# Edge gather of the second stream: every second indirect gather waits for the landing of the one ahead of it

## The chip, the cores and the metric

The kernel runs on one core of one Trainium2 chip. Its time is the device time of one execution in microseconds (us), smaller is better. The kernel before takes 4981.63 us, the median of three runs (4978.19 to 4985.81).

## The reference

The reference takes node features `x` (6250 nodes, 256 features), a list of 200000 edges for a first graph layer and a list of 131072 edges for a second one. Cut to what matters:

```python
xn = layernorm(x)
x  = x + graph_attention(xn, src, dst)            # 200000 edges, 4 heads of 64
       + linear_attention(xn)                      # 8 heads of 32
y  = layernorm(x)
h  = y @ W_gat                                     # 16 columns: 4 heads x 4 experts
e  = leaky_relu(a_src[src] + a_dst[dst])           # 131072 edges and one loop per node
alpha = exp(e - max over dst) / sum over dst
scores = layernorm(segment_sum(h[src] * alpha, dst) + b).mean over heads
out = x + sum over 4 experts of gate(scores) * (gelu(y @ W1[e] + b1[e]) @ W2[e] + b2[e])
```

The change concerns `h[src]` and `a_src[src]` of the second graph layer: one row of 20 numbers (16 of `h`, 4 of `a_src`) is fetched for every edge.

## The kernel before

The program runs through stages that follow one another. First the edges are sorted and tables built; then comes the first stream, which fetches a row of 264 numbers for each edge of the first graph with 1612 indirect gathers and sums them by destination. A third group of stages computes the nodes' features for the second layer and sorts its edges. Then comes the second stream (`edge_stream`, L2109 to L2401), and last the gates and the weighted sum of the experts.

The second stream works on 1216 chunks of 128 edges, in 38 bundles of `SPAN` = 32 chunks. For each chunk, GpSimd (POOL) issues one indirect gather (L1929) of 128 rows of 20 floats, one row to each partition, into a ring of `GATHERED` = 6 bundle slots in SBUF. Each slot has a semaphore of its own, `got[slot]`, which each landed gather raises by 16. POOL does nothing else in this stream: its whole program there is one call of `EdgeGather.share`. The first `AHEAD` = 112 gathers (3.5 bundles) are issued in the stage ahead of the stream by `EdgeGather.ahead`, which calls `share` in lots of 8; the other 1104 are issued in the stream itself (L2212).

Two waits hold POOL back in `share`. At the first chunk of a bundle it waits until the slot is free again, that is, until VectorE has done `scale` (L2335) of the bundle six back (semaphore `scaled`). And each gather of bundle `j` waits until all 32 gathers of bundle `j - 2` have landed.

What uses the rows: for each bundle, VectorE waits for `got[slot]` and adds the two scores (`pack`, L2311), TensorE turns them (L2221), VectorE runs the maximum over runs of equal destinations (`shift`, L2321 to L2328), ScalarE takes the exponential (L2276), TensorE turns back (L2228), ScalarE copies out (L2282), VectorE multiplies the gathered rows by the weights (`scale`, L2335), and TensorE sums the rows of each chunk with a one-hot matrix (L2238). VectorE then combines the chunks' sums (`align`, `combine`). Between these steps TensorE, ScalarE and VectorE work on a fixed list of steps of the four experts' dense layers (`Experts`, L2043 to L2106), 12 steps in each bundle; the order on each engine is written out by hand. SyncE loads the run marks (`resets`, L2184) and stores the experts' rows (L2023) and the states of each bundle (L2189).

Of the kernel before, what the change touches and what calls it, by code (L numbers as in the profile page):

```python
# [27 lines left out]
WIDE = E2 // P + BLOCK  # L28
SPAN = 32
GATHERED = 6  # L30
BUNDLES_AT_ONCE = 2
EDGE_CHUNKS = 1216
EDGE_GRID = 1280
# [1289 lines left out]
def stream(nc, kept, c, sem, d, g, e, x, wqkv, wout, gamma, key_max):  # L1323
# [8 lines left out]
    GAP = P - 1 + LOW  # L1332
    AT_ONCE = BUNDLES_AT_ONCE
    assert NB % AT_ONCE == 0
# [387 lines left out]
class UnitScatter:  # L1722
# [9 lines left out]
    def share(self, pool, n):  # L1732

        for u in range(self.done, self.done + n):
            lot, v = u // LOT, u - self.first
            if lot >= 2:
                pool.wait_ge(self.scattered[(lot - 2) % 3], 16 * LOT * ((lot - 2) // 3 + 1))
            pool.indirect_dma_start(  # L1738
                out=self.out, out_offset=bass.IndirectOffsetOnAxis(ap=self.unit[:, v:v + 1], axis=0),
                in_=self.keys[:, v * UNIT:(v + 1) * UNIT], in_offset=None, bounds_check=ROOM - 1,  # L1740
                oob_is_err=False).then_inc(self.scattered[lot % 3], 16)
        self.done += n
# [162 lines left out]
class EdgeGather:  # L1905


    def __init__(self, nc, kept, c, d, g, e):
        self.rows, self.src, self.chunks, self.done = d[g.tag + "_rows"], e.src, g.chunks, 0
        self.out = kept.enter_context(nc.sbuf_tensor(g.tag + "_gathered", [P, GATHERED, SPAN, 20], F32))  # L1910
        self.got = [c.held.enter_context(nc.semaphore("%s_rows_got%d" % (g.tag, k))) for k in range(GATHERED)]

# [7 lines left out]
    def share(self, pool, n, scaled=None):  # L1920

        end = min(self.chunks, self.done + n)
        for k in range(self.done, end):
            j, u = divmod(k, SPAN)
            if j >= GATHERED and u == 0:
                pool.wait_ge(scaled, j - GATHERED + 1)
            if j >= 2:
                pool.wait_ge(self.got[(j - 2) % GATHERED], 16 * SPAN * ((j - 2) // GATHERED + 1))
            pool.indirect_dma_start(out=self.out[:, j % GATHERED, u, :], out_offset=None, in_=self.rows,  # L1929
                                    in_offset=bass.IndirectOffsetOnAxis(ap=self.src[:, k:k + 1], axis=0)  # L1930
                                    ).then_inc(self.got[j % GATHERED], 16)
        self.done = end
# [924 lines left out]
```

## Time and profile before

| what | us |
|---|---|
| median of three runs | 4981.63 |
| the profiled execution, from its first to its last instruction (its span) | 6245.5 |
| busy in the profiled execution: TensorE matmul | 3399.7 |
| VectorE | 2946.1 |
| ScalarE | 1902.2 |
| GpSimd | 3158.9 |
| gathers of the first stream (L1440), busy, 1612 of them | 1603.5 |
| gathers of the second stream (L1929), busy, 1216 of them | 1201.9 |
| GpSimd idle just before gathers of L1929 | 1249.8 |

The profile is of one execution, and that one took 6245.5 us where the three timed runs took 4978 to 4986. The page shows no time for it but the span, so the span is its own time. A row of the page's groups gives the line, the engine, the operation, what it writes and reads, the count, then busy us and mean ns of one, then the idle time of the engine just before these instructions with what released it. The busy time of a gather on POOL is the making of its descriptors; when its data land is another time. PEclk is the granted clock of TensorE as a share of full speed.

### The profile page before, as it was taken

How to read it: one execution, taken by the hardware profiler on the slowest of the kernel's cores; microseconds unless marked ns; L12 is line 12 of the kernel's file. 1: busy time of each engine (PE TensorE's matmuls, PEld its weight loads, DVE VectorE, ACT ScalarE, POOL GpSimd, SP SyncE). 2: the span in 40 equal slices, each digit the busy share in tenths (PEclk: the TensorE clock that was granted, in tenths of full speed). 3: DMA queues.
4: the chain of work that ended last, by engine and by line, in shares of the span. 5: the costliest groups of instructions: out<-in, count | busy, mean ns of one | idle time of the engine just before them, and what ended most of it. 6: DMA issues, size and time to landing. Idle time of an engine off the chain costs nothing. (4 is left out here: it accounts for less than half of the span.)

```text
span 6245.5 us, 58318 instructions
## 1 busy us (share of the span) xinstructions
PE 3399.7 (54%) x14771; PEld 2497.0 (40%) x14771; DVE 2946.1 (47%) x6874; ACT 1902.2 (30%) x6108; POOL 3158.9 (51%) x3144
## 2 busy tenths in 40 slices
PE   5554356565666666655552634555455554555660
PEld 4454244444444444443342523334334343343450
DVE  8765455555566666665564722122222222222336
ACT  4100244444456566655441001111111111111220
POOL 0176666665666566656644673544444545445200
PEclk8655677777767777777765556677677776777765
DMA  3265333333333334333321631111111113334216
GB/s 109 74 207 166 104 93 95 95 96 91 95 101 106 105 106 109 106 100 96 93 76 52 223 109 24 26 26 27 24 25 31 23 30 24 25 31 22 30 34 248
DMA packets 326836, 508.54 MB, mean 81 GB/s; under 512 B 102092, under 2 KB 249219, under 8 KB 314654
## 3 DMA queue, kind: packets, MB, share of 16 engines
q0 software_dynamic: 126320, 232.73, 19.0%
q1 hardware_dynamic: 190334, 266.01, 13.0%
q10 hardware_dynamic: 9900, 6.68, 0.3%
q8 instruction: 100, 1.64, 0.1%
q14 instruction: 182, 1.48, 0.1%
HBM read 425.57 MB, written 79.71 MB: 81 GB/s over the span
## 5 line engine op out<-in xcount | busy, mean ns | idle before, releaser
L1440 POOL DMA_INDIRECT gnn_gathered<-gnn_rows,gnn_src x1612 | 1603.5, 995 | 970.2 <-issue 454.4
L1929 POOL DMA_INDIRECT ffn_gathered<-ffn_rows,ffn_src x1216 | 1201.9, 988 | 1249.8 <-DVE ffn_scaled L2335 807.9
L1528 PE MATMUL gnn_step_ps<-gnn_scaled,gnn_dst_onehot 128*128 128x260 f32 x3224 | 1209.8, 517 | 820.2 <-DVE gnn_scaled L1622 585.3
L1467 ACT ACTIVATE gnn_scaled<-gnn_gathered,gnn_edge_weights 128x65 f32<-128x65 f32 x4464 | 1137.4, 336 | 778.2 <-remote 377.5
L1528 PEld LDWEIGHTS gnn_step_ps<-gnn_scaled,gnn_dst_onehot 128*128 128x128 f32 x3224 | 746.7, 252 | 1122.6 <-DVE gnn_scaled L1622 674.2
L1642 DVE TENSOR_TENSOR gnn_sums<-gnn_sums,gnn_step_ps 128x260 f32 x1612 | 680.5, 422 | 623.9 <-PE gnn_step_ps L1528 252.0
L2054 PE MATMUL exp_hidden_ps<-exp_xn_turned,exp_w 128*128 128x512 f32 (+1 forms) x832 | 532.5, 777 | 486.4 <-ACT exp_hidden L2085 342.5
L2238 PE MATMUL ffn_sum_ps<-ffn_scaled,ffn_dst_onehot 128*128 128x24 f32 x2432 | 392.6, 320 | 350.6 <-issue 234.3
L2085 ACT ACTIVATE exp_hidden<-exp_hidden_ps,exp_b 128x512 f32<-128x512 f32 (+1 forms) x208 | 137.8, 663 | 1304.9 <-remote 750.5
L2238 PEld LDWEIGHTS ffn_sum_ps<-ffn_scaled,ffn_dst_onehot 128*128 128x128 f32 x2432 | 392.0, 254 | 356.5 <-issue 235.1
L2054 PEld LDWEIGHTS exp_hidden_ps<-exp_xn_turned,exp_w 128*128 128x128 f32 x832 | 189.8, 253 | 659.0 <-ACT exp_hidden L2085 365.6
L2062 PE MATMUL exp_out_ps<-exp_w,exp_hidden 128*128 128x256 f32 x1568 | 416.9, 414 | 0.0
L2062 PEld LDWEIGHTS exp_out_ps<-exp_w,exp_hidden 128*128 128x128 f32 x1568 | 341.9, 219 | 168.7 <-issue 126.0
L2305 DVE TENSOR_TENSOR ffn_dst_onehot<-ffn_local_dst,iota_row 128x1024 f32<-128x1024 f32 x152 | 183.0, 1224 | 430.2 <-DMA gnn_bundle_ends<-gnn_step_ends 322.8
L2106 DVE TENSOR_TENSOR exp_out<-exp_out_ps,exp_b 128x256 f32<-128x256 f32 x196 | 80.7, 421 | 487.0 <-PE exp_out_ps L2062 361.5
L1738 POOL DMA_INDIRECT ffn_keys<-edges_sorted,edges_unit_place x192 | 226.7, 1181 | 77.6 <-issue 57.7
L2074 ACT COPY exp_xn_turned<-exp_turn_ps 128x256 f32<-128x256 f32 x49 | 18.3, 372 | 769.2 <-PE exp_turn_ps L2043 767.6
L1558 DVE TENSOR_TENSOR gnn_dst_onehot<-gnn_local_dst,iota_row 128x1664 f32<-128x1664 f32 x124 | 236.7, 1909 | 0.1
L2321 DVE TENSOR_TENSOR_SCAN ffn_maximum_until<-ffn_resets_of_rows,ffn_row_ps 128x128 f32<-128x128 f32 x38 | 15.9, 418 | 416.3 <-remote 394.4
L1622 DVE TENSOR_TENSOR gnn_scaled<-gnn_gathered,gnn_edge_weights 128x260 f32<-128x260 f32 x496 | 209.6, 423 | 2.5 <-issue 1.2
L2348 DVE TENSOR_SCALAR ffn_missing<-ffn_sum_ps 128x64 f32<-128x64 f32 x76 | 16.8, 221 | 378.1 <-DMA gnn_bundle_ends<-gnn_step_ends 315.0
L1738 POOL DMA_INDIRECT ffn_keys<-mid_late_keys,mid_late_unit x102 | 113.3, 1110 | 87.8 <-DMA mid_late_unit<-late_unit 57.0
(424 smaller groups left out, 4469.6 us busy)
## 6 DMA issues: line engine op xcount, KB each, us to landing
nn_local_rows_everywhere<-gnn_local_rows SPq DMA_DIRECT2D x52, 1024.0 KB
fn_local_rows_everywhere<-ffn_local_rows SPq DMA_DIRECT2D x40, 1024.0 KB
gnn_gathered<-gnn_rows,gnn_src POOLq DMA_INDIRECT x1612
expert_rows<-exp_out SPq DMA_DIRECT2D x196, 128.0 KB
sum_expert_rows<-expert_rows SPq DMA_DIRECT2D x12, 2048.0 KB, 16.8
ffn_gathered<-ffn_rows,ffn_src POOLq DMA_INDIRECT x1216
ffn_kept_states<-ffn_states SPq DMA_DIRECT2D x38, 384.0 KB
mix_xn_transposed<-xn_transposed SPq DMA_DIRECT2D x98, 128.0 KB
```

The source lines that it names most:

```text
L1440: pool.indirect_dma_start(out=G[:, n, u, :], out_offset=None, in_=d[t + "_rows"], in_offset=bass.IndirectOffsetOnAxis(ap=e.src[:, st:st + ...
L1467: last = act.activation(ZW[:, st % BUF, h * F:(h + 1) * F], G[:, i % 2, u, h * F:(h + 1) * F], ACT.Copy, scale=W[:, i % 2, h, u:u + 1])
L1528: pe.matmul(ps[:, st % BUF, 0:g.row], OH[:, st // PIECE % 2, u % PIECE, :], ZW[:, st % BUF, :], start=True, stop=True).then_inc(multiplied, 1)
L1558: dve.tensor_tensor(OH[:, piece % 2], bcast(e.dst[:, cut].unsqueeze(2), [P, PIECE, P]), bcast(c.row[:].unsqueeze(1), [P, PIECE, P]), ALU.i ...
L1622: dve.tensor_tensor(ZW[:, st % BUF, :].rearrange("p (h f) -> p h f", h=H), G[:, i % 2, u, 0:g.row].rearrange("p (h f) -> p h f", h=H), bca ...
L1642: dve.tensor_tensor(to, to, ps[:, st % BUF, 0:g.row], ALU.add).then_inc(added, 1)
L1738: pool.indirect_dma_start(out=self.out, out_offset=bass.IndirectOffsetOnAxis(ap=self.unit[:, v:v + 1], axis=0), in_=self.keys[:, v * UNIT: ...
L1929: pool.indirect_dma_start(out=self.out[:, j % GATHERED, u, :], out_offset=None, in_=self.rows, in_offset=bass.IndirectOffsetOnAxis(ap=self ...
L2054: last = pe.matmul(self.PH[:, 0:w], self.W1[:, e, k, q * P:(q + 1) * P], self.XT[:, i % 2, k, 0:w], start=k == 0, stop=k == 1)
L2062: last = pe.matmul(self.PO[:, n % 2, 0:D], self.HT[:, e % 2, h, q * P:(q + 1) * P], self.W2[:, e, h, :], start=h == 0, stop=h == self.HC - 1)
L2238: last = pe.matmul(ps[:, u // HALF, u % HALF * COLS:(u % HALF + 1) * COLS], OH[:, u // PIECE % 2, u % PIECE, :], ZW[:, u, :], start=True, ...
L2305: dve.tensor_tensor(OH[:, q % 2], bcast(e.dst[:, cut].unsqueeze(2), [P, PIECE, P]), bcast(c.row[:].unsqueeze(1), [P, PIECE, P]), ALU.is_eq ...
```

## The change

Inside the second stream (where `scaled` is given), a gather at an even place `u` of its bundle now waits until the gather directly ahead of it, `k - 1`, has landed; the first of the stream is left out, since the one ahead of it belongs to the stage before. The gathers at odd places keep the wait on the bundle two back. The gathers of the stage ahead of the stream (`ahead`, which passes no `scaled`) are as they were. No instruction is added or removed on any other engine.

```diff
+PAIR = 2
...
             j, u = divmod(k, SPAN)
             if j >= GATHERED and u == 0:
                 pool.wait_ge(scaled, j - GATHERED + 1)
-            if j >= 2:
+            if scaled is not None and u % PAIR == 0 and k > self.done:
+                b, v = divmod(k - 1, SPAN)
+                pool.wait_ge(self.got[b % GATHERED], 16 * (SPAN * (b // GATHERED) + v + 1))
+            elif j >= 2:
                 pool.wait_ge(self.got[(j - 2) % GATHERED], 16 * SPAN * ((j - 2) // GATHERED + 1))
             pool.indirect_dma_start(out=self.out[:, j % GATHERED, u, :], out_offset=None, in_=self.rows,
                                     in_offset=bass.IndirectOffsetOnAxis(ap=self.src[:, k:k + 1], axis=0)
```

## Rows read from the trace of the kernel before

**Rows 1.** Busy time by stretch: us, then PE, PEld, DVE, ACT, POOL, PEclk, DMA share, GB/s.
```profile
0.00:622.00 622.00, 339.92 (x2804) 291.12 (x2804) 439.72 (x1032) 101.91 (x283) 240.13 (x213) 0.63 0.43 139
622.00:3172.00 2550.00, 1502.65 (x4896) 1069.54 (x4896) 1523.17 (x3794) 1313.23 (x4802) 1603.49 (x1612) 0.74 0.37 99
3172.00:3640.00 468.00, 226.23 (x2027) 193.58 (x2027) 303.98 (x676) 69.99 (x306) 248.89 (x215) 0.54 0.39 128
3640.00:5840.00 2200.00, 1147.85 (x4251) 798.29 (x4252) 481.74 (x944) 350.09 (x599) 1065.43 (x1103) 0.70 0.22 28
5840.00:6061.00 221.00, 183.01 (x795) 144.50 (x794) 92.55 (x178) 61.16 (x113) 0.97 (x2) 0.77 0.10 31
6061.00:6245.00 184.00, 0.00 (x0) 0.00 (x0) 104.99 (x252) 5.84 (x7) 0.00 (x0) 0.50 0.63 218
```

**Rows 2.** Waits on POOL: who waited for whom, us in total, times, longest us.
```profile
POOL ffn_gathered L1929 <- DVE ffn_scaled L2335: 807.9, 31, 46.8
...
POOL gnn_gathered L1440 <- DVE gnn_scaled L1622: 449.3, 154, 8.2
POOL ffn_gathered L1929 <- issue: 360.4, 1182, 0.3
```

**Rows 3.** The gathers by line: count, min/median/max ns, first and last start.
```profile
L1929 POOL DMA_INDIRECT ffn_gathered<-ffn_rows,ffn_src x1216: 941/947/1977, 3456.0 to 5840.3; - x174
...
L1440 POOL DMA_INDIRECT gnn_gathered<-gnn_rows,gnn_src x1612: 942/949/2653, 622.2 to 3171.1; - x180
```

**Rows 4.** The step `scale`, L2335: while gathers are issued, and after the last gather.
```profile
L2335 DVE TENSOR_TENSOR ffn_scaled<-ffn_gathered,ffn_edge_weights x32: 683/684/691, 3685.3 to 5800.3; 128x512 f32<-128x512 f32 x32
...
L2335 DVE TENSOR_TENSOR ffn_scaled<-ffn_gathered,ffn_edge_weights x6: 683/684/684, 5871.3 to 6040.6; 128x512 f32<-128x512 f32 x6
```

**Rows 5.** Timeline of one bundle's turn (start us, us, engine, line), POOL and DVE.
```profile
4535.70 0.95 POOL L1929 DMA_INDIRECT ffn_gathered<-ffn_rows,ffn_src  x1 [0.30 <-issue]
...
4558.78 0.69 DVE L2335 TENSOR_TENSOR ffn_scaled<-ffn_gathered,ffn_edge_weights 128x512 f32<-128x512 f32 x1
...
4559.74 0.94 POOL L1929 DMA_INDIRECT ffn_gathered<-ffn_rows,ffn_src  x1 [23.09 <-DVE ffn_scaled L2335]
...
4560.98 0.95 POOL L1929 DMA_INDIRECT ffn_gathered<-ffn_rows,ffn_src  x1 [0.30 <-issue]
```

**Rows 6.** Stretches behind the gather of 4535.70, columns as in rows 1.
```profile
4537.00:4537.50 0.50, 0.00 (x0) 0.00 (x0) 0.00 (x0) 0.00 (x0) 0.00 (x0) 1.00 0.22 17
4537.50:4537.80 0.30, 0.00 (x0) 0.00 (x0) 0.00 (x0) 0.00 (x0) 0.00 (x0) 0.57 0.05 7
4537.80:4541.00 3.20, 0.00 (x0) 0.00 (x0) 0.00 (x0) 0.00 (x0) 0.00 (x0) 0.50 0.00 0
```

**Rows 7.** Timeline: turned scores and `shift` beside gathers, then without gathers.
```profile
4514.35 0.27 PE L2221 MATMUL ffn_row_ps<-identity,ffn_scores 128*128 128x128 f32 x1
...
4541.50 0.42 DVE L2321 TENSOR_TENSOR_SCAN ffn_maximum_until<-ffn_resets_of_rows,ffn_row_ps 128x128 f32<-128x128 f32 x1 [20.48 <-remote]
4541.55 0.69 ACT L2085 ACTIVATE exp_hidden<-exp_hidden_ps,exp_b 128x512 f32<-128x512 f32 x1 [14.09 <-remote]
...
5921.79 0.27 PE L2221 MATMUL ffn_row_ps<-identity,ffn_scores 128*128 128x128 f32 x1
...
5922.17 0.42 DVE L2321 TENSOR_TENSOR_SCAN ffn_maximum_until<-ffn_resets_of_rows,ffn_row_ps 128x128 f32<-128x128 f32 x1 [3.31 <-PE ffn_row_ps L2221]
```

**Rows 8.** The last gather of all, and the stretches behind it.
```profile
5840.33 0.95 POOL L1929 DMA_INDIRECT ffn_gathered<-ffn_rows,ffn_src  x1 [0.30 <-issue]
...
5843.00:5843.50 0.50, 0.00 (x0) 0.00 (x0) 0.00 (x0) 0.00 (x0) 0.00 (x0) 0.50 0.76 12
5843.50:5844.00 0.50, 0.00 (x0) 0.00 (x0) 0.00 (x0) 0.00 (x0) 0.00 (x0) 0.50 0.01 0
5844.00:5845.00 1.00, 0.00 (x0) 0.00 (x0) 0.00 (x0) 0.00 (x0) 0.00 (x0) 0.50 0.00 0
```

**Rows 9.** Two stretches of 200 us of the second stream, columns as in rows 1.
```profile
4400.00:4600.00 200.00, 109.65 (x401) 76.82 (x401) 45.56 (x89) 32.75 (x56) 92.08 (x96) 0.70 0.13 26
...
5200.00:5400.00 200.00, 109.22 (x409) 76.11 (x410) 46.84 (x91) 33.90 (x61) 93.27 (x96) 0.72 0.46 26
```

## The prediction, made before the changed kernel was run

> **What bounds the kernel now.** I read the busy time by stretch first [rows 1]. The second stream's gathers fill 3640 to 5840: 2200 us, in which no engine is busy for more than 1148. The waits on POOL come next [rows 2]: it stood 807.9 us before 31 gathers until VectorE had done `scale`, which frees a slot of the ring. So in this trace the gathers are not late; the other engines are. The starts of `scale` say by how much [rows 4]: (5800.3 - 3685.3) / 31 = 68.2 us a bundle while gathers are issued, (6040.6 - 5871.3) / 5 = 33.9 us after the last one. The timeline shows where the difference lies [rows 7]. TensorE turned the scores at 4514.35 and VectorE's scan of them began at 4541.50, with ScalarE let go within 0.1 us of it, 5.8 us after POOL's last gather had started [rows 5]; without gathers the same hand-over took 0.38 us (5921.79 to 5922.17).
>
> Taken alone, this speaks for the change: space the bursts out, and the others run. But the profiled execution took 6245.5 us and the timed runs 4981.6, 1264 less, so not all of its stalls can be in the timed runs, and I have to find what they leave. Work outside the two streams' gathers: 622 + 468 + 184 [rows 1], and of the 221 us after the last gather about 48, one bundle's 33.9 and the closing steps, since six bundles had piled up only because the others were late: 1322 us. That leaves 4982 - 1322 = 3660 us. The first stream issues 1612 gathers, and from one to the next POOL needs 0.95 us of work and 0.30 of issue, 1.25 together (4559.74 to 4560.98) [rows 3, 5]: at least 2015 us. So the second stream's 1104 gathers have at most 3660 - 2015 = 1645 us, where the trace has 2200; at 1.25 us each they need at least 1380, or 40 us a bundle. Without the stalls the others need 33.9 us a bundle, less than POOL's 40. My reading is therefore that in the timed runs **POOL's issue paces the second stream**. Between the floors (2015 + 1380 = 3395) and 3660 lie 265 us that I can't place. I give the second stream 60 of them and the first the rest: the first has a ring of two bundles and POOL waits there for VectorE 154 times, 449.3 us [rows 2], and its VectorE, TensorE and ScalarE are busy 1523, 1503 and 1313 us [rows 1], while the second has six slots. So the second stream's gathers take about 1440 us now.
>
> The Trainium skill says otherwise of the two times: "Runtime: NRT & Kernel Launch", section on the preamble and postamble, has a gap of about 6.2 us between a profile's total and the reported time, whatever the kernel. By it the timed runs would hold all the stalls of the trace. The gap here is 1264 us, so the measurement decides against it; what the stalls would mean if they were real is the second rival below.
>
> **The change part by part.** It removes the wait on the bundle two back from 551 gathers (even places, numbers 114 to 1214). That wait never held: no group of POOL's waits at L1929 names a landing [rows 2], so its removal is worth nothing. The 0.30 us between gathers stays. The 112 gathers of the stage ahead are untouched.
>
> It adds 551 waits for the landing of the gather just issued. What stands behind each on POOL is only the next gathers; who waits for those is `pack` on VectorE, and through it the whole bundle. The price of a pair:
>
> - From the even gather to the odd one nothing changes: 1.25 us.
> - From the start of the odd gather to its landing. The gather that started at 4535.70 is the last of a burst with the other transfers quiet. DMA work goes on through 4537.50 and into the next 0.3 us, and is nil from 4537.80 [rows 6]: landing 1.8 to 2.1 us after the start. For the stores of the experts' rows and states that run beside some gathers I take 2.1.
> - From the landing to POOL's next start. The nearest row is a wait for VectorE: `scale` ended at 4558.78 + 0.69 = 4559.47 and POOL started at 4559.74 [rows 5]: 0.27.
>
> Together 1.25 + 2.1 + 0.27 = 3.62 us, where two gathers take 2.50 now. A bundle then takes 16 x 3.62 = 57.9 us on POOL. The others need 33.9, and they are hidden behind it; if TensorE, with longer pauses, were granted the lower of its clocks (0.50 in idle stretches of rows 6) they would need more, but 24 us of cover are left. The lead of 3.5 bundles is used up either way. Nothing late is cured, since nothing on the other engines is late in the timed runs.
>
> The sum: 552 pairs x 3.62 = 1998 us, less 1440, is +558. The landings can't all be at the quiet value, so I round up to +570: 4982 + 570 = **about 5550 us**. Against the profiled execution's own 6245.5 the sum is another: its 68.2 us a bundle would be replaced by 57.9 if the spaced gathers no longer hold the others up, 10.3 x 34.5 = 355 us less, and by about the same 68 if they do. I expect a span of 5900 to 6400 there, a profile that looks equal or better beside timed runs that are worse.
>
> Bounds of the unknown terms. The wait can't cost less than nothing if the landing came with the end of the descriptors (1.25 + 0.95 + 0.27 = 2.47 a pair, against 2.50), and no row has a landing so early. Above: the last gather of all started at 5840.33 and DMA work goes on until about 5843.5 [rows 8], a landing after 3.1 us; and from 5200 us on the DMA share is 0.46 for the same 26 GB/s that had 0.13 before [rows 9], so landings were longer there. With 3.1 a pair takes 4.62, 2550 us in all, +1110. I stay near the quiet value because two thirds of the stream's stretch have it.
>
> The trace shows the landing at 2.0 us with the DMA engines at 0.05 to 0.22 of their time [rows 6] and 3.1 with them at 0.76 [rows 8]. The Trainium skill, "DMA: Bandwidth & Descriptors", section on latency, has the access to HBM at 0.2 us on average and 2 us at high load, and says that lighter load makes the fixed cost smaller. By that rule the spaced gathers would see shorter landings; what this gives is the third rival.
>
> **The rivals.**
>
> 1. *Long landings.* The state of rows 9 (share 0.46 for the same bytes) belongs to the chip and not to the trace, and holds for a third of the stream or more: 184 pairs x 1.0 us more, +184 and up, with all pairs +552: 5730 to 6100, say 5850. For it: those rows. Against it: the row at 4400 has the same load at 0.13. Chance 0.12.
> 2. *The stalls are real, and the change cures them* (the other side). If the bursts hold TensorE's results back in the timed runs too, a bundle takes more than POOL's 40 us now, and it decides from where it takes more than 57.9. At the trace's 68.2 against 57.9 the change brings 355 us: 4630. For it: [rows 4, 7]. Against it: 68.2 x 34.5 = 2350 us doesn't fit into the 1645 left, unless POOL's work on a gather is also drawn out in the trace; then both streams shrink in proportion (3660 / 4750 = 0.77), 68.2 becomes 52.5, and 57.9 becomes 44.6: 270 us less, 4710. Chance 0.08.
> 3. *Short landings.* With nothing recorded and only two gathers under way, the landing comes 1.5 us after the start, midway between the 0.95 us of descriptors and the 2.1: 3.02 a pair, 1667 us, +227: 5210 (up to 5300 with 1.6). For it: a landing gets shorter where the DMA engines are idle [rows 6, 8]. Against it: rows 6 is already idle. Chance 0.15.
> 4. *It does nothing.* The timed runs' bundle is held at about 58 us by something that no row shows, and POOL's new pace hides behind it: 4980. For it only the 265 us that I couldn't place; against it that 58 x 34.5 = 2000 exceeds 1645. Chance 0.04.
>
> **How the numbers follow.** The forecast has 0.61 and its own range is 5400 to 5700 (landings of 1.85 to 2.35 us: 552 x 0.25 = 138 to either side, rounded up). Rivals 1 and 3 lie on the same side of no change, so the range takes in most of both: 5230 to 5850. Beyond it are rivals 2 and 4 and the far end of 1, about 0.18. Slower by over 0.2% (10 us, about what timing of this kernel can tell from nothing): 0.61 + 0.12 + 0.15 = 0.88. Faster: 0.08. Within 0.2%: 0.04.
>
> **What the profile after would show.** If I am right: POOL's starts at L1929 come in pairs 3.5 to 3.7 us long; its idle time there is put down mostly to landings of `ffn_gathered`, 551 times at 1.3 to 1.6 us, some 800 us; the 807.9 us of waits for `scale` shrink to less than 400; and `pack` (L2311) waits for gathers in bundles after the third. The rest of the kernel, first stream included, stays as it is. I would be wrong at the pair's price if the pairs in the trace last over 4.2 or under 3.1 us. I would be wrong in the reading of the timed runs if they come out under 5000: then the stalls of rows 7 were theirs too. The same is shown if the timed difference is much less than the pairs' sum.

## The result, and the profile after

The changed kernel took 5928.27 us (5925.25 to 5941.01, 4 runs), the kernel before beside it 4979.91 (4971.53 to 4985.81): ratio 1.1913, interval 1.1891 to 1.1936. That is 948 us slower. The forecast was 5550, 570 slower; the direction was right, and the time lies above the range of 5230 to 5850. A ratio is taken over all the runs of a series but those over 1.5% above the fastest, so it can differ a little from the quotient of the two medians.

Everything below needs one fact first. The series were run on several chips, and **the chips are of two kinds for this kernel**. The kernel before took 4979.91, 4976.24 and 4973.44 us in three series and 6369.83, 6254.88 and 6263.32 in three others. Ratios are always taken within one series. I call them the quick and the slow chips. Each of the five series below had a chip of its own and stayed on one of the two levels throughout; that it is the chip, and nothing else that differed between the series, is the plainest reading and was not tested by itself. The result above is from a quick chip. The profiled execution of before (6245.5) fits a slow one.

The profile after spans 5939.0 us, and that same execution was timed at 5941.01. The waits on POOL, columns as in [rows 2]:
```profile
POOL ffn_gathered L1933 <- DMA ffn_gathered<-ffn_rows,ffn_src: 1153.7, 551, 5.9
POOL gnn_gathered L1441 <- issue: 419.1, 1375, 0.3
...
POOL ffn_gathered L1933 <- issue: 202.0, 663, 0.3
...
POOL gnn_gathered L1441 <- DVE gnn_scaled L1623: 68.0, 67, 1.7
```
All 551 added waits held, 2.09 us each, where I had foreseen 1.3 to 1.6. The 807.9 us of waits for `scale` are gone, and so are most of the 449.3 us in the first stream, which the change doesn't touch. That second fact can't come from the edit.

The gathers by line, as in [rows 3], and then, from the page's list of DMA issues, their median us from issue to landing:
```profile
L1933 POOL DMA_INDIRECT ffn_gathered<-ffn_rows,ffn_src x1216: 939/945/2299, 3108.8 to 5713.1; - x174
...
L1441 POOL DMA_INDIRECT gnn_gathered<-gnn_rows,gnn_src x1612: 941/947/2672, 606.7 to 2825.1; - x180
```
```profile
ffn_gathered<-ffn_rows,ffn_src POOLq DMA_INDIRECT x1216, 2.5
```
The same time for the gathers issued from 3295 to 4900 us alone, then from 5000 to 5713:
```profile
DMA to landing us min/median/max: 2.2/2.4/7.0
```
```profile
DMA to landing us min/median/max: 3.1/3.2/5.1
```
Pairs in the timeline of POOL, as in [rows 5], and two stretches, columns as in [rows 1]:
```profile
4302.19 0.94 POOL L1933 DMA_INDIRECT ffn_gathered<-ffn_rows,ffn_src  x1 [1.64 <-DMA ffn_gathered<-ffn_rows,ffn_src]
4303.44 0.94 POOL L1933 DMA_INDIRECT ffn_gathered<-ffn_rows,ffn_src  x1 [0.30 <-issue]
4306.09 0.94 POOL L1933 DMA_INDIRECT ffn_gathered<-ffn_rows,ffn_src  x1 [1.70 <-DMA ffn_gathered<-ffn_rows,ffn_src]
```
```profile
4200.00:4400.00 200.00, 104.58 (x409) 73.59 (x408) 48.65 (x99) 33.34 (x57) 96.58 (x99) 0.70 0.14 26
5400.00:5600.00 200.00, 106.47 (x411) 78.97 (x411) 44.04 (x85) 32.05 (x55) 79.23 (x80) 0.68 0.16 24
```
This pair takes 3.90 us, of which 2.65 go from the odd gather's start to the next start, where I had 2.1 + 0.27. Over 200 us there are 99 gathers in the one stretch (4.04 us a pair) and 80 in the other (5.0): the late part of the stream is slower. After this odd gather, of 4303.44, the last DMA work shows between 4305.4 and 4305.6, and POOL starts again at 4306.09 (columns as in [rows 1]):
```profile
4305.40:4305.60 0.20, 0.00 (x0) 0.00 (x0) 0.00 (x0) 0.00 (x0) 0.00 (x0) 1.00 0.02 3
4305.60:4305.80 0.20, 0.00 (x0) 0.00 (x0) 0.00 (x0) 0.00 (x0) 0.00 (x0) 1.00 0.00 0
```
`pack` now waits for gathers in 32 bundles, 1229.6 us in all, as foreseen. The second stream runs from 3295.05 to 5713.1, 2418 us; I had 1998.

The hand-over of [rows 7], TensorE's turned scores to VectorE's scan: what VectorE stood before it, us and times, in all 38 bundles.
```profile
  PE ffn_row_ps L2225: 11.3, 3
```

### The profile page after: what moved, and what is told of

Its sections match the earlier page's. It is cut to its first block and busy times, and to the rows that moved or that the text cites. A ratio compares the mean times of both kernels' runs of the same rounds, so it can differ in the third digit from the quotient of the medians.

```text
span 5939.0 us, 58318 instructions
## 1 busy us (share of the span) xinstructions
PE 3176.8 (53%) x14771; PEld 2356.0 (40%) x14771; DVE 2929.5 (49%) x6874; ACT 1890.0 (32%) x6108; POOL 3276.4 (55%) x3144
## 5 line engine op out<-in xcount | busy, mean ns | idle before, releaser
L1933 POOL DMA_INDIRECT ffn_gathered<-ffn_rows,ffn_src x1216 | 1238.1, 1018 | 1433.5 <-DMA ffn_gathered<-ffn_rows,ffn_src 1153.7
L1441 POOL DMA_INDIRECT gnn_gathered<-gnn_rows,gnn_src x1612 | 1680.4, 1042 | 546.4 <-issue 419.1
L1529 PE MATMUL gnn_step_ps<-gnn_scaled,gnn_dst_onehot 128*128 128x260 f32 x3224 | 1109.9, 481 | 633.8 <-DVE gnn_scaled L1623 536.5
L1529 PEld LDWEIGHTS gnn_step_ps<-gnn_scaled,gnn_dst_onehot 128*128 128x128 f32 x3224 | 685.6, 232 | 909.6 <-DVE gnn_scaled L1623 645.0
L2315 DVE TENSOR_TENSOR ffn_score_sums<-ffn_gathered,ffn_dst_score_of_edge 128x128 f32<-128x128 f32 x38 | 15.8, 415 | 1229.8 <-DMA ffn_gathered<-ffn_rows,ffn_src 1229.6
L2225 PE MATMUL ffn_row_ps<-identity,ffn_scores 128*128 128x128 f32 x38 | 17.2, 453 | 1032.6 <-DVE ffn_scores L2319 1032.6
L2058 PE MATMUL exp_hidden_ps<-exp_xn_turned,exp_w 128*128 128x512 f32 (+1 forms) x832 | 491.3, 724 | 29.5 <-ACT exp_hidden L2089 17.2
L2242 PEld LDWEIGHTS ffn_sum_ps<-ffn_scaled,ffn_dst_onehot 128*128 128x128 f32 x2432 | 367.9, 243 | 8.9 <-DVE ffn_scaled L2339 6.6
L2242 PE MATMUL ffn_sum_ps<-ffn_scaled,ffn_dst_onehot 128*128 128x24 f32 x2432 | 365.8, 311 | 6.0 <-DVE ffn_scaled L2339 6.0
```

Of the source, the lines that this page charges most:

```text
L1441: pool.indirect_dma_start(out=G[:, n, u, :], out_offset=None, in_=d[t + "_rows"], in_offset=bass.IndirectOffsetOnAxis(ap=e.src[:, st:st + ...
L1529: pe.matmul(ps[:, st % BUF, 0:g.row], OH[:, st // PIECE % 2, u % PIECE, :], ZW[:, st % BUF, :], start=True, stop=True).then_inc(multiplied, 1)
L2058: last = pe.matmul(self.PH[:, 0:w], self.W1[:, e, k, q * P:(q + 1) * P], self.XT[:, i % 2, k, 0:w], start=k == 0, stop=k == 1)
L2242: last = pe.matmul(ps[:, u // HALF, u % HALF * COLS:(u % HALF + 1) * COLS], OH[:, u // PIECE % 2, u % PIECE, :], ZW[:, u, :], start=True, ...
```

## The experiments

**First series, a quick chip** (before: 4976.24, 4966.23 to 4994.33). *e1_before_again* is the kernel before with nothing changed, for its profile.

> The kernel before, unchanged, for a second profile of it. The trace of the changed kernel has its span at its timed value (5939 us against 5928) and its first stream 346 us shorter than the trace of before (gathers from 607 to 2825, against 622 to 3171), though the first stream is the same code. Theory A (in the timed runs POOL's issue paces the second stream): a trace at the timed value of 4980 us has the 1104 gathers of the second stream at 1.25 to 1.35 us each, 1380 to 1490 us from first to last (5941 - 2418 for the changed kernel's stretch = 3523 for the rest, and 4980 - 3523 = 1457), VectorE's scan L2321 follows TensorE's L2221 within about 1 us, and POOL waits little for ffn_scaled. Theory B (the stalls of the first profile are in the timed runs as well): the stretch is near 2200 us again and POOL waits about 800 us for ffn_scaled L2335.

*e2_every_fourth*:
```
-PAIR = 2
+PAIR = 4
```


> The wait for the gather ahead stands at every fourth gather (275 waits) instead of every second (551). Theory A (each wait exposes one landing and the restart of POOL, and POOL paces the stream): in the changed kernel a pair took 4.08 us up to gather 880 and 4.9 us behind it, 1.58 and 2.4 us over 2.50, so half the waits cost half of the sum: 188 x 1.58 + 88 x 2.4 = 508, less the slack of about 75 us that the kernel before has on POOL: 4980 + 430 = 5410, between 5370 and 5480. Theory C (the price is set by how few gathers are under way, not by the number of waits): the two of four that are under way at once still leave the DMA engines idle and the time stays over 5700.

*e3_three_back* (against the changed kernel; two counters for each slot, filled by alternate pairs, and `pack` waits for both):
```
...
-            if scaled is not None and u % PAIR == 0 and k > self.done:
-                b, v = divmod(k - 1, SPAN)
+            if scaled is not None and u % PAIR == 0 and k - 2 > self.done:
+                b, v = divmod(k - 3, SPAN)
...
```


> Same count of waits as in the change (550), each for the landing of the gather three back instead of the one ahead (each bundle slot gets two semaphores so that the wait is exact; pack waits for both). Theory A (what costs is the exposed landing): the gather three back started 3.75 us earlier, and landing takes 2.1 to 2.9 us and the restart about 0.5, so the wait holds POOL almost nowhere: 4980 us, at most 60 us more from the filler gathers at the end of the stream. Theory D (any wait on a landing stops POOL's sequencer and costs its restart, however far back the gather): 550 x about 0.5 us, 5200 us or more, up to the 5928 of the change.

*e4_no_landing_wait* (against the kernel before):
```
-            if j >= 2:
+            if j >= 2 and scaled is None:
```


> The kernel before without the wait on the bundle two back inside the second stream (only the ring's wait for ffn_scaled is left there). Theory A: that wait never holds, the time is the same within 0.3%, 4965 to 4995 us. Rival E: the wait on two bundles back throttles POOL in the filler gathers of the last third or protects the other engines: then the time moves by more than 20 us, in either direction.

Measured: e1 4987.12 (one run, span 4985.2); e2 5481.05, ratio 1.1015 (1.0986 to 1.1044); e3 5018.24, 1.0072 (1.0046 to 1.0097); e4 4976.15, 0.9997 (0.9984 to 1.0009).

e1, gathers by line with what the engine idled for, then POOL's waits:
```profile
L1929 POOL DMA_INDIRECT ffn_gathered<-ffn_rows,ffn_src x1216: 940/944/3306, 3102.5 to 4758.6; - x174
...
  issue: 370.0, 1214
```
```profile
POOL gnn_gathered L1440 <- issue: 422.5, 1387, 0.3
...
POOL gnn_gathered L1440 <- DVE gnn_scaled L1622: 71.1, 64, 1.9
```
There is no wait for `scale` at all: POOL goes from gather to gather with only the 0.30 us of issue. From 3288.41 to 4758.6 it needs 1470 us for the 1104 gathers, 1.33 each, where I had 1440. So on this kind of chip the reading "POOL's issue paces the stream" is shown, and 2418 - 1470 = 948 us, the whole difference of the result. e4 shows that the removed wait was worth nothing on such a chip. e3 keeps just as many landing waits, each two gathers older; of those, only 97 still held:
```profile
POOL ffn_gathered L1934 <- DMA ffn_gathered<-ffn_rows,ffn_src: 59.2, 97, 3.5
```
It costs 42 us, not 948. The price is the exposed landing and not the wait instruction. In e2, 275 waits held:
```profile
POOL ffn_gathered L1933 <- DMA ffn_gathered<-ffn_rows,ffn_src: 600.4, 275, 5.6
```
505 / 275 = 1.84 us a wait, beside 948 / 551 = 1.72 in the change: the cost goes with the number of exposed landings. The 5481 of e2 lies at the end of its expected range (5370 to 5480).

**Second series** asked why the late pairs are longer; in the profile after they lengthen at about gather 875 (3.9 to 4.0 us before it, 4.7 to 5.1 from 880 on). The reference's edge list runs over 8192 node numbers, of which 6250 exist, so only about 100000 edges are kept, and by the program's sorting the row numbers from about gather 856 on are filler, all 0: the 128 descriptors of a gather read one row. No run read the row numbers out; e5 and e7 test them by their effect. It fell on a slow chip (before: 6369.83, 6317.7 to 6431.77). *e5_change_spread_rows*, and *e6_before_spread_rows* the same edit in the kernel before:
```
-                                    in_offset=bass.IndirectOffsetOnAxis(ap=self.src[:, k:k + 1], axis=0)
+                                    in_offset=bass.IndirectOffsetOnAxis(ap=self.src[:, k - 400 * (k >= 832):k - 400 * (k >= 832) + 1], axis=0)
```


> The change, but from chunk 832 on the gathers take the row numbers of the chunk 400 ahead of them, so that each fetches 128 different real rows; the chunks from about 856 on hold filler edges, whose row numbers are all 0, so all 128 descriptors of such a gather read one row. (The kernel so computes with other rows for some real edges of chunks 832 to about 856.) In the changed kernel a gather took 2.03 to 2.07 us up to chunk 880 and 2.40 to 2.49 behind it. Theory F (128 reads of one address land later): the tail runs at 2.04 too, 336 gathers x 0.42 = 141 us less: 5790 us, 5770 to 5815. Theory G (what is slow in the tail has to do with the place in the stream, the tables or the time): unchanged, 5928.

> The same other row numbers from chunk 832 on in the kernel before. There nothing waits closely for a landing: both theories have the time unchanged at 4976 within 0.3%, while by theory F the landings of the last third (3.6 us behind the start, by the transfers' records of the second profile) fall to 2.1 to 2.3 and the DMA share there falls back to that of the middle; by theory G they stay. If the time falls by more than 15 us, the filler gathers cost POOL something in the kernel before as well (its descriptors took 1.03 to 1.08 us there, 1.02 elsewhere).

*e7_change_one_row*: the changed kernel, the second stream's `self.src[:, k:k + 1]` always column 1215, filler. *e8_wait_at_every_gather*: `PAIR = 1`.

> The change with every gather of the stream (from 112 on) fetching the filler chunk's row numbers, so that all gathers read one row 128 times (the sums of the second layer are computed from the wrong rows). Theory F: each of the 756 gathers ahead of the tail costs 2.46 us instead of 2.04, +318: 6245 us. Theory G: 5928 still.

> The wait for the gather ahead at every gather, 1103 waits. Theory A (each wait exposes the landing and costs about the same, whatever the others do): a lone gather is 2.55 to 2.65 us from start to next start in the first two thirds and 3.4 in the tail: 756 x 2.6 + 348 x 3.4 = 3149 us against 1470, so 4976 + 1680 = 6655 us, 6550 to 6800. If the price per wait grew because two gathers landed together in the change (theory H: of a pair's landing, part is queueing behind the first one), the landing of a lone gather is shorter, 2.2 us or less from start to start: below 6300.

Measured: e5 6233.57, 0.9802 (0.9749 to 0.9855); e6 6369.96, 1.0000 (0.9958 to 1.0042); e7 6683.27, 1.0499 (1.043 to 1.0567); e8 7296.65, 1.1462 (1.1393 to 1.1531). Stretches of e5, then of e7, columns as in [rows 1]:
```profile
4200.00:4400.00 200.00, 106.96 (x413) 74.71 (x411) 45.73 (x89) 33.44 (x57) 99.26 (x101) 0.70 0.13 27
5400.00:5600.00 200.00, 106.84 (x406) 74.98 (x407) 49.14 (x101) 32.74 (x56) 98.99 (x100) 0.69 0.13 26
```
```profile
4200.00:4400.00 200.00, 105.25 (x399) 75.66 (x398) 41.39 (x74) 32.74 (x56) 80.29 (x82) 0.67 0.17 25
```
With real rows the late stretch is as quick as the early one (100 and 101 gathers); with filler the early one is as slow as the late one was (82). The longer landing of 128 reads of one row is shown, 0.8 us a pair; the landings of 2.4 and 3.2 us in the profile after say the same. In e8 each of 1103 waits held, 2226.8 us in all, and its second stream took 3304 us, 1.66 us a wait over the 1470 of e1. e5 and e6 fetch other rows for the real edges from gather 832 on too, and e7 fetches the filler's rows for every edge of the stream, so none of the three computes the reference's sums.

e5 and e7 were told as ratios to a before of about 4976, and here the before was 6370. e6's POOL rows show what is different on such a chip:
```profile
POOL ffn_gathered L1929 <- DVE ffn_scaled L2335: 804.0, 31, 47.1
POOL gnn_gathered L1440 <- DVE gnn_scaled L1622: 521.7, 152, 8.0
```
They are [rows 2] again, and this kernel's timed runs are at 6370 too. The stalls are in timed runs here. So the change itself had to be run on a slow chip.

**Third series, a slow chip** (before: 6254.88, 6209.82 to 6296.62): the change, `PAIR = 4`, and e5 and e6 once more.

> The change, unchanged. The same kernel before took 4976 us on the chip of the first experiments and 6370 us on that of the second ones, and the change with spread rows came out 2.0% faster than the kernel before there. Where the kernel before takes about 4976: 5928 again. Where it takes about 6370: the pair of gathers is as long as ever (2.04 us a gather, 2.45 in the filler tail), so the change is the spread version (6233) plus 336 x 0.42 = 141: 6375 us, no different from the kernel before (theory J: the change puts a pace of 65 us a bundle in the place of stalls that cost as much). If the landing waits cost more there (theory K), it is over 6450.

> The wait at every fourth gather. Where the kernel before takes 4976: 5481 again. Where it takes 6370, POOL's pace would be 54.3 us a bundle (62 in the tail) against the 66 at which the kernel before runs. Theory L (what holds TensorE's results back is a long unbroken row of gathers; any gap lets them through): 34.5 x 11 = 380 us less, less the pile-up at the end that goes too: 5850 to 6000 us. Theory M (it goes by the gathers' mean rate, and at 54 us a bundle they are still held back): 6200 us or more.

> The change with 128 different rows in place of the filler's one row. Where the kernel before takes 4976: 5928 - 141 = 5787 us (5770 to 5815), the same 141 us that the gathers' pace in the tail (2.03 us instead of 2.45) gave in the profile of its first run. Where it takes 6370: 6233 again.

> The kernel before with 128 different rows in the tail. Where the kernel before takes 4976: POOL's descriptors set the pace and the landings are hidden, 4976 within 0.3%; landings of the last third fall from 3.6 to about 2.1 us. Where it takes 6370: 6370 again.

Measured: f1 6273.16, **1.003** (0.9993 to 1.0067); f2 5854.24, **0.9381** (0.9286 to 0.9476); f3 6160.92, 0.9841 (0.9754 to 0.9927); f4 6249.8, 0.9992 (0.9953 to 1.0031). f1 was expected at 6375 and f3 at 6233, both worked out from the chip of the second series, which is slower still. The gathers of f1 by line, and POOL's waits:
```profile
L1933 POOL DMA_INDIRECT ffn_gathered<-ffn_rows,ffn_src x1216: 938/945/2405, 3442.7 to 6041.2; - x174
```
```profile
L1441 POOL DMA_INDIRECT gnn_gathered<-gnn_rows,gnn_src x1612: 940/947/2658, 609.8 to 3158.9; - x180
```
```profile
POOL ffn_gathered L1933 <- DMA ffn_gathered<-ffn_rows,ffn_src: 1150.9, 551, 5.5
...
POOL gnn_gathered L1441 <- DVE gnn_scaled L1623: 435.1, 150, 7.9
```
The changed second stream costs POOL the same on both kinds (1150.9 us of landings here, 1153.7 there). What f1 has over the profile after is the untouched first stream: 2549 against 2218 us, 331 of the 345 between the two medians. Against the kernel before on such a chip [rows 3], the second stream has 2414 us (3627 to 6041) in place of 2200, and after the last gather come 227 us in place of 405, since no bundles pile up: +214 - 178 = +36 of some 6260, close to the +18 measured. In f4 the late stretch has DMA share 0.13, where the filler rows of [rows 9] had 0.46 for the same 26 GB/s, yet the time is the same; there the landings are hidden.
```profile
5400.00:5600.00 200.00, 110.17 (x406) 76.63 (x407) 46.08 (x90) 34.43 (x62) 93.38 (x96) 0.70 0.13 26
```

**Fourth series, a slow chip** (before: 6263.32, 6250.23 to 6283.69): `PAIR = 8` (h1) and `PAIR = 16` (h4), the kernel of e3 (h2), and h3, the kernel before with the gathers from the seventh bundle on cut to 64 of 128 partitions (`self.out[0:64, ...]`, `self.src[0:64, ...]`), which leaves the other half of the rows stale.

> The landing wait at every eighth gather, 137 waits. Where the kernel before takes 4976: 137 x 1.84 = 250 more, 5225. Where it takes about 6250: POOL's pace would be 48.5 us a bundle. Theory L (any gap lets TensorE's results through): 34.5 x 6 = 200 us less than with every fourth (5854): 5650. Theory N (only short rows do, results are held after about 8 us of unbroken gathers, as in the first profile): stalls come back and the time is over 5850.

> The landing wait at every sixteenth gather, 69 waits. Where the kernel before takes 4976: 5100. Where it takes about 6250: theory L 5550 (POOL's pace 45.6 us a bundle); theory N near 6000 to 6250.

> 550 waits for the gather three back. Where the kernel before takes 4976: 5018 again. Where it takes about 6250: by the rate of gathers, which these waits leave as it is (1.34 us a gather), nothing is let through, 6250; if the mere presence of a landing wait in POOL's queue were what helps, below 5900.

> The kernel before, but in the stream every gather from bundle 6 on fetches rows for partitions 0 to 63 alone, so half the row transfers with the same number of gathers and of semaphore increments (the other half of the rows is left stale). Where the kernel before takes about 6250: theory Q (what is in the way is the traffic of row transfers and their descriptors): stalls all but go, below 5700. Theory R (it is the gathers and their semaphore increments as such): stalls stay, within 200 us of 6250. Where it takes 4976: POOL's descriptors get shorter, and the stream ends at the 34 us a bundle that the other engines need: 4980 - 31 x 9 = 4700, or 4976 if a gather's 1.3 us do not depend on its rows.

Measured: h1 5606.24, **0.8969** (0.8927 to 0.9011); h4 5955.92, 0.9462 (0.9368 to 0.9556); h2 6166.95, 0.9859 (0.9801 to 0.9918); h3 6215.68, 0.9929 (0.9901 to 0.9957). POOL's waits in h1, h4 and h2:
```profile
POOL ffn_gathered L1933 <- DMA ffn_gathered<-ffn_rows,ffn_src: 321.2, 132, 5.6
```
```profile
POOL ffn_gathered L1933 <- DVE ffn_scaled L2339: 421.3, 24, 28.4
...
POOL ffn_gathered L1933 <- DMA ffn_gathered<-ffn_rows,ffn_src: 104.4, 43, 5.0
```
```profile
POOL ffn_gathered L1934 <- DVE ffn_scaled L2341: 710.8, 31, 45.5
```
And what VectorE stood before the scan of [rows 7], in e6 (no gaps), in h4 (one gap in sixteen) and in h1 (one in eight):
```profile
  remote: 343.7, 20
```
```profile
  remote: 80.7, 17
```
```profile
  PE ffn_row_ps L2225: 14.6, 5
```
The scan's is one hand-over of several. ScalarE's wait for TensorE's results of the experts (`exp_hidden`) in the second stream's gathers, in before, h4, h3 and h1 (`remote`: the view names no instruction that let it go):
```profile
ACT exp_hidden L2085 <- remote: 750.5, 39, 32.9
```
```profile
ACT exp_hidden L2089 <- remote: 633.9, 44, 42.0
```
```profile
ACT exp_hidden L2085 <- remote: 546.8, 26, 41.5
```
```profile
ACT exp_hidden L2089 <- PE exp_hidden_ps L2058: 549.0, 129, 20.4
```
So on a slow chip TensorE's results are handed over late while gathers are issued in long rows, and a landing wait in every eighth gather ends nearly all of it. One in sixteen ends most of the scan's delay but little of ScalarE's, and its time lies between the two that were expected (5550; 6000 to 6250). Below eight the gaps themselves become the bound again. Each wait of h1 costs POOL 321.2 / 132 = 2.43 us, and its bundles take 48 to 51 us (52 to 55 in the filler) in place of 65 in the mean. Waits three back (h2) help by 1.4% only, again between what was expected (6250; below 5900). Only 51 of them held, 40 of these in the filler from gather 880 on, and there alone its bundles are shorter: 55 to 63 us, where before has 63 to 71. With half the rows in each gather (h3) the kernel still stands at 0.993, and POOL waits 801.9 us for `scale` as before, though the scan's own `remote` wait is down to 62.3 us. So what counts is the number of gathers and not the bytes, and the scan's wait alone is a poor measure of the stalls.

**Fifth series, a quick chip** (before: 4973.44, 4971.55 to 4976.47). *i1_both_streams_eighth*: `PAIR = 8`, and in the first stream
```
+                    if st and u % PAIR == 0:
+                        b, v = divmod(st - 1, S)
+                        pool.wait_ge(got[b % 2], 16 * (S * (b // 2) + v + 1))
```
*i2_pause_no_wait*: the kernel before, with a pause of POOL that waits for no landing (the wait is for the pause before it):
```
+            if scaled is not None and u % 8 == 0:
+                if self.paused:
+                    pool.wait_ge(self.rested, self.paused)
+                pool.memset(self.idle[:], 0.0).then_inc(self.rested, 1)
+                self.paused += 1
```


> Landing waits at every eighth gather of the second stream, as before, and at places 0, 8, 16 and 24 of each bundle of 26 in the first stream (247 more). Its gathers move 13 times the bytes, so a wait there costs 2 us or more. Where the kernel before takes about 6260: the first stream's gathers took 2620 us there and 2211 us where the kernel takes 4976; the waits cost 247 x 2 = 494 us of POOL's time and can give back up to 409: about 5690 us, between 5550 and 5800, no gain over 5606. If the first stream's stalls are of another kind, 6000 or more. Where the kernel before takes 4976: 5225 + 450 = 5675.

> The kernel before with a memset of 128 x 1024 floats on POOL ahead of every eighth gather of the second stream (138 of them), into a tile that nothing reads, and no new landing wait. A memset of about 1 us and the hand-over leave a pause of some 1.5 us between gathers, in which the last gather lands only in part. Where the kernel before takes about 6260: if a pause of POOL is what lets the results through, about 5600 to 5700; if the gathers have to have landed, 5950 or more. Where it takes 4976: 138 x 1.5 = 207 more, 5180.

Measured: i1 5790.21, 1.1646 (1.1623 to 1.1668); i2 5084.65, 1.0224 (1.0204 to 1.0244). POOL's waits in i1 and its timeline in i2:
```profile
POOL gnn_gathered L1444 <- DMA gnn_gathered<-gnn_rows,gnn_src: 527.2, 201, 3.8
...
POOL ffn_gathered L1936 <- DMA ffn_gathered<-ffn_rows,ffn_src: 324.5, 137, 5.1
```
```profile
4001.55 0.94 POOL L1936 DMA_INDIRECT ffn_gathered<-ffn_rows,ffn_src  x1 [0.30 <-issue]
4002.49 0.97 POOL L1932 MEMSET ffn_idle<- 128x1024 f32 x1
4003.62 0.95 POOL L1936 DMA_INDIRECT ffn_gathered<-ffn_rows,ffn_src  x1 [0.16 <-issue]
```
Both were meant for a slow chip and fell on a quick one, where there is no stall to cure. They show the costs alone: an exposed landing in the first stream (201 of them, 2.62 us of POOL's idle time each, where I had expected 2) and a pause of 0.8 us (111 / 138, where I had 1.5). Whether a pause without a wait frees a slow chip was not measured.

## Why the prediction was wrong, by its own steps

- **"In the timed runs POOL's issue paces the second stream", about 1440 us.** Right for the chip of the result: 1470 (e1), and the first stream has 2212 there where the sum leaves it 2220.
- **The removed wait is worth nothing.** Right on a quick chip: e4, 0.9997.
- **551 added waits, a landing exposed in each.** Right: 551 in the profile after. e3 shows that the landing is what costs.
- **Start of the odd gather to its landing, 2.1 us: the step that failed.** This term of the pair's price was too small for every pair. I took it from the last activity of the DMA engines [rows 6]. In the profile after that activity ends at about 2.1 us as well (4303.44 to 4305.5), but POOL starts again only 0.5 us later and not 0.27. With real rows a gather lands 2.4 us after its issue in the median (2.2 at the least), and from the odd gather's start to the next start the median is 2.65 where I had 2.37. Over 551 waits that is 154 us. In the filler the landing takes 3.2 us.
- **"The landings can't all be at the quiet value", rounded up by 12 us, and the upper bound of 3.1 given to a third of the stream only as rival 1.** The mean wait was 2.09 us where my sum has 1.42 (2.37 - 0.95): 369 us over 551 waits. Of these, 154 are the step above, about 145 the filler rows (168 pairs at 4.93 us against 4.08; e5 and e7), and the other 70 single longer landings, some 30 of them in the first four bundles; what lengthens those no run took apart. The descriptors, at 0.99 us in the mean and not 0.95, add 44. 369 + 44 = 413 of the 420 by which the stream's 2418 exceeds 1998. The forecast itself missed by less, 378, since the stream had 1470 before and not 1440 and I had rounded up by 12. [Rows 9] had shown the filler stretch, and I read it as a rival instead of as a term. The 3.1 us of [rows 8] is a filler gather too: I put its length down to the share of 0.76, and it is what filler takes at 0.16. Rival 1's time (5730 to 6100) was the right one, and its mechanism in half: the long landings are real for a third of the stream, but they belong to the row numbers and not to the chip.
- **Rival 3, short landings.** Wrong: the least one is 2.2 us. The rule of the Trainium skill ("DMA: Bandwidth & Descriptors", latency) that lighter load on HBM makes the fixed cost smaller found no support, as far as the gathers' own load goes: real rows land after 2.4 us in the median with one, two or four gathers under way (e8, the profile after, e2). In e5 and e7 the bytes moved are alike (27 and 25 GB/s), and which row is read makes the difference.
- **"Not all of its stalls can be in the timed runs."** The conclusion held and the reason did not. I took 6245.5 against 4981.6 as profile against timed run; it was one kind of chip against another. The profile after and its own timed value differ by 2.0 us (5939.0, 5941.01), e1's by 1.9. The Trainium skill's rule ("Runtime: NRT & Kernel Launch", preamble and postamble), which I set aside on the strength of those 1264 us, fits in that the two agree within a few us. It puts the profile's total 6.2 us above the reported time; the span used here is 2 us below it, so the 6.2 itself is not shown.
- **Rival 2, the stalls are real and the change cures them.** The stalls are real on a slow chip: f1 1.003 there in place of 1.19. The change cures them and pays about as much in landings (its bundles take 70 us in the mean, not 57.9), so its 4630 was nowhere, and the outcome is that of rival 4, no change. A thinner dose wins: h1, 0.8969, is faster than the kernel before and the changed one on such a chip, and 657 us faster than the first. On a quick chip no version that was run beat the kernel before; `PAIR = 8` and `PAIR = 16` were not run there.
- **Checks named ahead.** Pairs over 4.2 us as a sign of a wrong price: they were 4.04 early and 5.0 late, 4.38 in the mean, so that sign spoke as meant. The span of 5900 to 6400 came out at 5939.0, but by accident: it was worked out for a slow chip, where f1 had 6268.3. That the first stream stays as in the profile before failed, since that profile is of the other kind of chip.

**Open:** what differs between the two kinds of chip; whether the gap alone, the landing in it or the lower rate of gathers frees TensorE's hand-over; why the first stream is 331 us longer on a slow chip.

## What to carry to other kernels

Price a wait for a transfer by the time from issue to landing as the waiting engine sees it, not by the last byte moved, and price it for every stretch of the data separately; padding that reads one address is a stretch of its own. Where an in-order queue of transfers is the bound, each exposed landing is paid in full (1.7 to 1.8 us on a quick chip), and has to bring more than that elsewhere; a wait two gathers older costs next to nothing. When a profile and the timed runs differ by a quarter, profile again before reasoning on either, and settle for a version only after it has been timed on both kinds of chip.

## What the runs showed of the hardware that was not expected

- The same program takes 4973 to 4980 or 6255 to 6370 us by the series, each on a chip of its own, and the difference is in stretches where POOL issues gathers back to back: e1's second stream 1470 us, a slow chip's 2200.
- On a slow chip, one landing wait in eight gathers takes 10.3% off the kernel; every second takes nothing, every fourth 6.2%, every sixteenth 5.4%.
- An indirect gather of 128 rows lands 2.4 us after its issue with real row numbers and 3.2 when all 128 descriptors read the same row (medians, profile after; 0.8 us a pair between e5 and e7).
